# Output projection by head pairs in seven block products, probabilities divided before rounding, values two heads later

## The chip, the core and the metric

The kernel runs on one core of a Trainium2 chip. Its engines work side by side, each through its own list of instructions: TensorE (PE) multiplies matrices, VectorE (DVE), ScalarE (ACT) and GpSimd (POOL) work element by element, SyncE (SP) issues the DMA transfers. They wait for each other by semaphores. SBUF is the memory on the chip, PSUM the eight banks into which TensorE writes. The metric is the time of one execution on the device, in microseconds.

## The reference, cut to what matters

A layer of latent attention and a gated feed-forward block (FFN) on an input of 8 x 512 x 512, in fp32, with random weights. Each of the 8 batches is independent:

```
x = x + attention(layernorm(x))
x = x + ffn(layernorm(x))
# attention, 16 heads, D_QK = 128 + 64, D_V = 128
q  = rmsnorm(h @ wq_a.T, q_norm_w) @ wq_b.T                # rope on the last 64 of each head
kv = h @ wkv_a.T;  kv_c = rmsnorm(kv[..., :128]);  k_pe = rope(kv[..., 128:])
k_nope, v = split(kv_c @ wkv_b.T)
attn = softmax(q @ k.T / sqrt(192))
out  = (attn @ v) @ wo.T                                    # 2048 -> 512
# ffn, 512 -> 1536 -> 512, weights rounded to fp8
down(silu(gate(x)) * up(x))
```

## The kernel before

Every operand is held as two f16 halves, a high one (rounded) and a low one (the rest), and a product is three matmuls: high by high, high by low, low by high (`mul3`, L287 to 293). The kernel never forms keys or values of a head: the key half of `wkv_b` is multiplied into the query weights (`WAB`, "absorbed"), the value half into `wo` (`WVO`, 16 matrices of 128 x 512), so all heads share one latent key and value of 128 columns, and what the softmax weights is the latent row ("context").

A batch has 4 tiles of 128 rows and 16 heads. In head i (`head_step`) TensorE computes the scores of head i (20 matmuls of 512 columns into four PSUM banks), the values of head i - 1 (12), the absorbed queries of head i + 2 (9) and the projection of head i - 1 (12, `project_out`). VectorE takes the four row maxima of the scores (L1427, `maxima`), copies the context of head i - 1 out of PSUM and splits it (L1441, L1222), adds the four projected tiles into the residual `XR` times the reciprocal of the row's sum (L1449), and makes the low half of a query (L1222). ScalarE computes each tile's exponential twice, in fp32 with its sum (L1077) and in f16 (L1079), and GpSimd subtracts the one from the other (L1716). SyncE turns the f16 halves with transposing DMAs, and the values of a head wait for them. The order on every engine is written out in the code; a loop runs over pairs of heads in the middle. Between the attentions lies the FFN, with the next batch's queries and keys prepared beside it. Statistics and the norm of the next batch's rows are spread over the middle heads (`next_norm`). The latent products of the next batch (`latent`) stand between the last heads.

The change and the prediction touch: `scores`, `values`, `project_out`, `attention`, `end_of_attention` on TensorE; `probs`, `attention` on ScalarE; `context`, `add_out`, `head_step`, `attention`, `last_of_attention` on VectorE; `head`, `next_norm`, `attention` on GpSimd; `batch` on SyncE.

## Time and profile before

| | |
|---|---|
| time, median of 3 runs | 2231.03 us (2230.93 to 2232.12) |
| the profiled execution's span, first to last instruction | 2228.8 us, 2.2 us below the median |
| TensorE busy | 2205.4 us, 99%, 10977 matmuls |
| VectorE busy | 1557.8 us, 70% |
| ScalarE busy | 1066.6 us, 48% |
| GpSimd busy | 1001.5 us, 45% |
| share of TensorE in the chain that ended last | 93% |
| granted TensorE clock, mean | 0.999 of full speed |

Matmuls overlap: each is recorded with 379 ns for 512 columns, but one follows the other sooner, and what counts is the distance between two starts. In the timeline a row is: start, duration, engine, line, operation, output and inputs, shapes, and, in brackets, how long the engine had been idle before and what released it. `x4` joins four instructions of the same kind that follow without a gap; the duration is then that of the run.

### The profile page before, as it was taken

Reading aid. Unit: us, or ns where it says so; the run is one execution under the profiler, and the core shown is the slowest. Engines: PE = TensorE matmul, PEld = TensorE weight load, DVE = VectorE, ACT = ScalarE, POOL = GpSimd, SP = SyncE. Lnnn points to the kernel's source line nnn. Section 1 sums busy time; section 2 is a strip of 40 time slices with the busy share of each in tenths; the row PEclk is TensorE's granted clock in tenths of the full one; section 3 lists DMA queues with packets and bytes.
Section 4 is the critical chain, followed back from the end, with each engine's and each line's share of the span. In section 5 each row is a group of like instructions: output and inputs, shape, how many; then the busy total and the mean of one; then the engine's idle time right before and its main releaser. Section 6 shows DMA issues by size and latency. Waiting matters only on the chain.

```text
span 2228.8 us, 34908 instructions
## 1 busy us (share of the span) xinstructions
PE 2205.4 (99%) x10977; PEld 1026.8 (46%) x10977; DVE 1557.8 (70%) x3227; ACT 1066.6 (48%) x2345; POOL 1001.5 (45%) x688
## 2 busy tenths in 40 slices
PE   7999999999999999999999999999999999999999
PEld 5444544445444454444544445444454445444454
DVE  7888887776477764777648775587755877467773
ACT  6667564554255542555325553355443554345532
POOL 4657465453355524454244642536334363343322
PEclk9999999999999999999999999999999999999999
DMA  7868336562175631756216561365614564145530
GB/s 248 188 124 150 88 71 142 106 124 51 23 151 105 122 53 34 145 105 127 44 43 146 106 121 29 73 123 106 118 25 104 106 115 95 24 104 109 106 65 19
DMA packets 703800, 219.42 MB, mean 98 GB/s; under 512 B 685520, under 2 KB 685776, under 8 KB 702672
## 3 DMA queue, kind: packets, MB, share of 16 engines
q1 hardware_dynamic: 703696, 218.09, 47.7%
q8 instruction: 59, 0.97, 0.2%
q14 instruction: 45, 0.37, 0.0%
HBM read 40.78 MB, written 8.39 MB: 22 GB/s over the span
## 4 chain that ended last, share of the span: by engine, by line
PE 93%; DVE 3%; ACT 1%; DMA 1%; POOL 1%; issue 1%; SPq 0%; DVEq 0%; POOLq 0%
PE bank L853 13%; PE bank L291 11%; PE bank L293 11%; PE bank L292 11%; PE scores L863 7%; PE scores L663 5%; PE scores L293 5%; PE scores L291 5%; PE scores L292 5%; PE bank L674 4%; PE bank L675 4%; PE bank L676 4%; PE scores L660 3%; PE bank L840 1%; PE bank L689 1%; PE scores L557 1%
## 5 line engine op out<-in xcount | busy, mean ns | idle before, releaser
L1716 POOL TENSOR_TENSOR arena<-arena 128x1024 f16<-128x1024 f32 x256 | 545.7, 2132 | 620.3 <-ACT arena L1079 620.3
L1077 ACT ACTIVATE arena<-scores,shift 128x512 f32<-128x512 f32 x512 | 357.5, 698 | 535.0 <-DVE shift L1429 494.8
L1449 DVE SCALAR_TENSOR_TENSOR arena<-bank,rden,arena 128x512 f32<-128x512 f32 x508 | 347.9, 743 | 137.0 <-PE bank L293 137.0
L1427 DVE TENSOR_REDUCE mx<-scores 128x1 f32<-128x512 f32 x512 | 352.5, 689 | 20.5 <-PE scores L293 16.7
L1079 ACT ACTIVATE arena<-scores,shift 128x512 f16<-128x512 f32 x512 | 358.6, 700 | 0.0
L853 PE MATMUL bank<-arena,WFF 128*128 128x512 f16 x1392 | 313.5, 379 | 0.8 <-DVE arena L1601 0.6
L1774 POOL TENSOR_TENSOR arena<-arena 128x512 f16<-128x512 f32 x96 | 114.4, 1191 | 255.6 <-ACT arena L1152 255.6
L853 PEld LDWEIGHTS bank<-arena,WFF 128*128 128x128 f16 x1392 | 135.9, 98 | 164.1 <-DVE arena L1601 2.3
L291 PE MATMUL bank<-WVO,arena 128*128 (+1 forms) x512 | 194.2, 379 | 2.4 <-DVE arena L1222 1.2
L1222 DVE SCALAR_TENSOR_TENSOR arena<-bank,arena 128x512 f16<-128x512 f32 (+1 forms) x263 | 176.2, 670 | 29.1 <-ACT arena L1070 24.4
L663 PE MATMUL scores<-arena 128*128 128x512 f16 x512 | 195.4, 382 | 0.0
L292 PE MATMUL bank<-WVO,arena 128*128 (+1 forms) x512 | 194.1, 379 | 0.0
L291 PE MATMUL scores<-arena 128*128 128x512 f16 x512 | 194.0, 379 | 0.0
L292 PE MATMUL scores<-arena 128*128 128x512 f16 x512 | 194.0, 379 | 0.0
L293 PE MATMUL scores<-arena 128*128 128x512 f16 x512 | 194.0, 379 | 0.0
L293 PE MATMUL bank<-WVO,arena 128*128 (+1 forms) x512 | 194.0, 379 | 0.0
L674 PE MATMUL bank<-arena 128*128 128x512 f16 x476 | 180.4, 379 | 1.9 <-DMA arena<-arena 1.7
L676 PE MATMUL bank<-arena 128*128 128x512 f16 x476 | 180.4, 379 | 0.0
L675 PE MATMUL bank<-arena 128*128 128x512 f16 x476 | 180.4, 379 | 0.0
L1441 DVE TENSOR_SCALAR arena<-bank 128x512 f16<-128x512 f32 (+1 forms) x135 | 89.0, 660 | 130.1 <-PE bank L676 125.7
L863 PE MATMUL scores<-WFF,arena 128*128 128x512 f16 x752 | 177.6, 379 | 0.0
L1601 DVE SCALAR_TENSOR_TENSOR arena<-arena,bank 128x512 f32<-128x512 f32 x96 | 65.9, 687 | 158.5 <-ACT arena L1146 158.4
(159 smaller groups left out, 3480.5 us busy)
## 6 DMA issues: line engine op xcount, KB each, us to landing
arena<-arena SPq DMA_TRANSPOSE x712, 3.2
arena<-w_ffn SPq DMA_DIRECT2D x24, 384.0 KB, 3.5
arena<-x SPq DMA_DIRECT2D x8, 1024.0 KB, 5.6
out<-arena SPq DMA_DIRECT2D x32, 256.0 KB, 2.0
arena<-x SPq DMA_DIRECT2D x14, 512.0 KB, 4.4
WVO<-w_o SPq DMA_DIRECT2D x4, 1024.0 KB, 8.2
arena<-w_nope SPq DMA_DIRECT2D x4, 768.0 KB, 9.1
arena<-down_scale SPq DMA_DIRECT2D x8, 256.0 KB, 3.3
```

What stands on the lines that cost most here:

```text
L291: pe.matmul(dst, lhsT=ls(0), rhs=rs(0), start=first, stop=False)
L292: pe.matmul(dst, lhsT=ls(0), rhs=rs(1), start=False, stop=False)
L293: return pe.matmul(dst, lhsT=ls(1), rhs=rs(0), start=False, stop=last)
L663: pe.matmul(dst, lhsT=Q1[:, par, tile(t)], rhs=KA[:, :], start=False, stop=False)
L674: pe.matmul(dst[:, :], lhsT=KV[:, 0, j, :], rhs=PT[:, par, 0, :, j, :], start=(j == 0), stop=False)
L853: m = pe.matmul(dst[:, :], lhsT=w[:, c, k, :], rhs=XT[:, p, k, :], start=(k == 0 and p == 0), stop=(k == NK - 1 and p == 1))
L863: m = pe.matmul(SC[:, t, :], lhsT=FU[:, c % 4, p, tile(t)], rhs=WD[:, c, :], start=(c == 0 and p == 0), stop=(c == NF - 1 and p == 1))
L1077: act.activation(P32[:, t, :], SC[:, t, :], ACT.Exp, scale=EXP_SCALE, bias=shift[:, t:t + 1], accum_out=esum[:, par, t:t + 1]).then_inc(s[ ...
L1079: act.activation(PH[:, par, t, :], SC[:, t, :], ACT.Exp, scale=EXP_SCALE, bias=shift[:, t:t + 1]).then_inc(s["ph"], 1)
L1427: dve.tensor_reduce(mx[:, t:t + 1], SC[:, t, :], AX_X, ALU.max).then_inc(s["mxr"], 1)
L1449: dve.scalar_tensor_tensor(out=XR[:, t, :], in0=banks[t][:, :], scalar=by[:, t:t + 1], in1=XR[:, t, :], op0=ALU.mult, op1=ALU.add).then_in ...
L1716: pool.tensor_tensor(PL[:, par, two, :], P32[:, two, :], PH[:, par, two, :], ALU.subtract).then_inc(s["pl"], 1)
```

## The change

From batch 2 on (`B_PLAIN = 2`), heads 0 to 13 form seven pairs. For a pair the contexts of the even head (E) and the odd one (O) stand side by side against their two weight matrices stacked; rows are cut in two (tiles 0, 1 and tiles 2, 3), the output columns in two. That is a product of 2 x 2 blocks by 2 x 2 blocks, and it is computed by seven block products and sums of blocks (Winograd's form of Strassen's method) instead of eight. A block product (`duo_product`) is two tiles by three matmuls of 256 columns. Heads 14 and 15 keep the old projection.

- The sums of weight blocks (T1 to T4) are computed once, on GpSimd in batch 1 (`block_sums`), split into halves, and written to DRAM with the plain blocks (`w_duo`); from then on each pair's seven blocks are read from there, four early and three late (`early_blocks`, `late_blocks`), into the space of the old matrices.
- The sums of context blocks (S1 to S4) are made on GpSimd in the odd heads (`context_sums`).
- Since contexts of two heads are added, the probabilities must be divided by their sums first. ScalarE now computes four exponentials (fp32), VectorE the reciprocals, and ScalarE then scales them: three tiles are copied twice (f16 and fp32, in place), the fourth is multiplied on GpSimd (`nm3`) and copied once (`probs_divided`, `head_divided`).
- The context leaves PSUM in fp32 (`context_rows`), ScalarE makes its f16 half (`context_hi`), VectorE the low half (`context_lo`).
- VectorE adds eight blocks of 128 x 512 elements a pair into `XR` (`add_block`).
- Values of head i - 2, not i - 1, are computed in head i, and scores wait for the fp32 exponentials (`ex`) alone.
- From batch 1 on the norm of the next batch's rows is done on VectorE (`next_rows`) and rounded on ScalarE (`next_rows_hi`), where GpSimd did both.
- TensorE's and ScalarE's loops over pairs are written out.

```diff
+B_PLAIN = 2
+N_DUO = NH // 2 - 1
+HB = H // 2
+N_BLK = 7
+W_B11, W_B21, W_T1, W_T2, W_T3, W_T4, W_B22 = range(N_BLK)
+N_EARLY = 4
+X_E1, X_O1, X_O2, X_S3, X_S1, X_S2, X_S4 = range(N_BLK)
+EARLY = [(X_E1, W_B11, 0, True), (X_O1, W_B21, 2, True), (X_S1, W_T1, 1, True), (X_S2, W_T2, 0, False)]
+LATE = [(X_S3, W_T3, 0, False), (X_S4, W_B22, 1, False), (X_O2, W_T4, 2, True)]
+ADDS = [(0, 0, 0), (2, 0, 0), (1, 1, 1), (0, 0, 1), (0, 1, 0), (0, 1, 1), (1, 0, 1), (2, 1, 0)]
...
+            def duo_head(b, i):
+
+                if i < NH - 2:
+                    sp.wait_ge(s["sp"], NT * (b * NH + i) + NT)
+                    rope_rows(i + 2, i % 2)
+                if i >= 2:
+                    sp.wait_ge(s["ctp"], b * N_CT + i - 1)
+                    sp.sem_inc(s["turn"])
+                for half in range(2):
+                    prob_rows_hi(b * NH + i, i % 2, half)
+                    prob_rows_lo(b * NH + i, i % 2, half)
...
+                    if b >= B_PLAIN and 0 < pair * 2 + par < NH - 1:
+                        pe.wait_ge(s["ex"], g * NT + (t - NT + 1))
...
+            def duo_product(j, x, w, k, start):
+
+                for t in range(2):
+                    dst = DBANK[k][:, t * HB:(t + 1) * HB]
+                    for m, (p, q) in enumerate(((0, 0), (0, 1), (1, 0))):
+                        r = pe.matmul(dst, lhsT=XP[j % 2][:, p, x, tile(t)], rhs=WB[:, q, w, :],
+                                      start=(start and t == 0 and m == 0), stop=(m == 2), skip_group_check=True)
+                return r
+
+            def duo_early(b, j, parts=(0, 1)):
+
+                n, base = (b - B_PLAIN) * N_DUO + j + 1, order_of_duo(b, j)
+                for k, (x, w, bk, start) in enumerate(EARLY):
+                    if (k > 0) not in parts:
+                        continue
+                    if k == 0:
+                        pe.wait_ge(s["w_early"], 16 * n)
+                        pe.wait_ge(s["ctl"], b * N_CT + 2 * j + 2)
+                        pe.wait_ge(s["outr"], base)
+                    if x == X_S1:
+                        pe.wait_ge(s["x_lo"], n)
+                    if x == X_O1:
+                        pe.wait_ge(s["cth"], b * N_CT + min(2 * j + 3, 2 * N_DUO))
+                    if x == X_S2:
+                        pe.wait_ge(s["outr"], base + 1)
+                    duo_product(j, x, w, bk, start).then_inc(s["outp"], 1)
+
+            def duo_late(b, j):
+
+                n, base = (b - B_PLAIN) * N_DUO + j + 1, order_of_duo(b, j)
+                pe.wait_ge(s["w_late"], 16 * n)
+                pe.wait_ge(s["outr"], base + 4)
+                for k, (x, w, bk, start) in enumerate(LATE):
+                    if x == X_O2:
+                        pe.wait_ge(s["cth"], b * N_CT + min(2 * j + 4, 2 * N_DUO))
+                    duo_product(j, x, w, bk, start).then_inc(s["outp"], 2 if x == X_S3 else 1)
+
+            def duo_step(b, i):
+
+                scores(b, i // 2, i % 2)
+                if i >= 2:
+                    values(b, i // 2 - 1, i % 2)
+                if i >= 4 and i % 2 == 0:
+                    duo_early(b, (i - 4) // 2, (0,))
+                absorb(i + 2, b * NH + i + 2)
+                if i >= 4 and i % 2 == 0:
+                    duo_early(b, (i - 4) // 2, (1,))
+                elif i >= 5:
+                    duo_late(b, (i - 5) // 2)
...
+            def probs_divided(b, i):
+
+                g, par, n = b * NH + i, i % 2, (b - B_PLAIN) * (2 * N_DUO) + i
+                for t in range(NT):
+                    act.wait_ge(s["shift"], NT * g + t + 1)
+                    if i > 0 and t % 2 == 0:
+                        act.wait_ge(s["pl"], 2 * g - 1 + t // 2)
+                    act.activation(P32[:, t, :], SC[:, t, :], ACT.Exp, scale=EXP_SCALE, bias=shift[:, t:t + 1],
+                                   accum_out=esum[:, par, t:t + 1]).then_inc(s["ex"], 1)
+                for t in range(NT):
+                    if t % 2 == 0:
+                        act.wait_ge(s["rdn"], 2 * n + 1 + t // 2)
+                        if i >= 2:
+                            act.wait_ge(p_t[par][t // 2], halves_landed(b, i))
+                    act.wait_ge(s["ex"], NT * g + t + 1)
+                    if t == NT - 1:
+                        act.wait_ge(s["nm3"], n + 1)
+                        act.activation(PH[:, par, t, :], P32[:, t, :], ACT.Copy).then_inc(s["ph"], 1)
+                    else:
+                        act.activation(PH[:, par, t, :], P32[:, t, :], ACT.Copy,
+                                       scale=rden_duo[:, par, t:t + 1]).then_inc(s["ph"], 1)
+                        act.activation(P32[:, t, :], P32[:, t, :], ACT.Copy,
+                                       scale=rden_duo[:, par, t:t + 1]).then_inc(s["nm"], 1)
+                    if t == 1 and i >= 2:
+                        context_hi(b, i - 2)
...
+            def context_rows(b, i):
+
+                n, j, par = b * N_CT + i, i // 2, i % 2
+                dve.wait_ge(s["ctp"], n + 1)
+                k = (b - B_PLAIN) * N_DUO + j
+                if par == 0 and k > 0:
+                    dve.wait_ge(s["x_sum"], 5 * k)
+                if par and k > 0:
+                    dve.wait_ge(s["x_lo"], k)
+                x = X32[:, X_O1:X_O2 + 1] if par else XE
+                dve.tensor_scalar(x, BC[:, :].rearrange("p (m n) -> p m n", m=2), 1.0 / NS, None,
+                                  ALU.mult).then_inc(s["cth"], 1)
+
+            def context_lo(b, i):
+
+                j, par = i // 2, i % 2
+                dve.wait_ge(s["x_hi"], (b - B_PLAIN) * 2 * N_DUO + i + 1)
+                if par:
+                    x = slice(X_O1, X_O2 + 1)
+                    dve.tensor_tensor(XP[j % 2][:, 1, x], X32[:, x], XP[j % 2][:, 0, x], ALU.subtract).then_inc(s["ctl"], 1)
+                else:
+                    dve.tensor_tensor(XP[j % 2][:, 1, X_E1], XE[:, 0], XP[j % 2][:, 0, X_E1],
+                                      ALU.subtract).then_inc(s["ctl"], 1)
...
+                bk, i, n = ADDS[k]
+                to = XR[:, 2 * i:2 * i + 2, n * HB:(n + 1) * HB]
+                dve.scalar_tensor_tensor(out=to, in0=DBANK[bk][:, :].rearrange("p (t n) -> p t n", t=2),
+                                         scalar=1.0 / (KS * VS), in1=to, op0=ALU.mult, op1=ALU.add).then_inc(s["outr"], 1)
...
+            def duo_adds(b, j, ks):
+                for k in ks:
+                    add_block(b, j, k)
+
+            def duo_step(b, i, part=None):
+
+                g = b * NH + i
+                maxima(g)
+                reciprocals(b, i)
+                if i >= 2:
+                    context_rows(b, i - 2)
+                if i >= 4 and i % 2 == 0:
+                    duo_adds(b, (i - 4) // 2, (0,))
+                if i >= 2:
+                    context_lo(b, i - 2)
+                if part in (0, 1, 2):
+                    next_norm(b, part)
+                if i >= 4 and i % 2 == 0:
+                    duo_adds(b, (i - 4) // 2, (1, 2, 3))
+                elif i >= 5:
+                    duo_adds(b, (i - 5) // 2, (4, 5, 6, 7))
+                qa_lo(g + 2, i % 2)
+                if part in (2, 3):
+                    next_norm(b, part + 1)
...
+            def head_divided(b, i):
+
+                g, par, n = b * NH + i, i % 2, (b - B_PLAIN) * (2 * N_DUO) + i
+                pool.wait_ge(s["ex"], NT * g + NT)
+                pool.wait_ge(s["rdn"], 2 * n + 2)
+                t = NT - 1
+                pool.tensor_tensor(P32[:, t, :], P32[:, t, :], rden_duo[:, par, t:t + 1].broadcast_to((P, S)),
+                                   ALU.mult).then_inc(s["nm3"], 1)
+                if i >= 3 and i % 2:
+                    context_sums(b, (i - 3) // 2)
+                for half in range(2):
+                    two = slice(2 * half, 2 * half + 2)
+                    pool.wait_ge(s["nm"], 3 * n + 2 + half)
+                    if half:
+                        pool.wait_ge(s["nm3"], n + 1)
+                    pool.wait_ge(s["ph"], NT * g + 2 * half + 2)
+                    pool.tensor_tensor(PL[:, par, two, :], P32[:, two, :], PH[:, par, two, :],
+                                       ALU.subtract).then_inc(s["pl"], 1)
+                    if i == 0:
+                        rotate(b, N_ROT_FFN + 1 + half)
+                if i >= 3 and i % 2:
+                    context_sums_rest(b, (i - 3) // 2)
...
+                x = [X32[:, m] for m in range(N_BLK)]
+                step(x[X_S1], XE[:, 1], x[X_O2], ALU.add, 0)
+                step(x[X_S3], XE[:, 0], XE[:, 1], ALU.subtract, 0)
+                step(x[X_S2], x[X_S1], XE[:, 0], ALU.subtract, 1)
+                step(x[X_S4], x[X_O1], x[X_S2], ALU.subtract, 3)
```

How the lists of instructions change, at three places. Names: `sp` scores done, `ex` exponential done, `ctp` values done, `outp` projected block done, `outr` block added, `qah` query's high half done, `x_hi` context's f16 half done, `x_lo` context sums split, `rdn` reciprocals done.

VectorE in a middle head before, after its four maxima (`bank` is PSUM, `arena` SBUF):

```order
L1434 TENSOR_SCALAR dsum<-esum 128x4 [waits ex]
L1436 RECIPROCAL rden<-dsum 128x4 [waits den]
L1441 TENSOR_SCALAR arena<-bank 128x512 [waits ctp]
L1222 SCALAR_TENSOR_TENSOR arena<-bank,arena 128x512 [waits cth]
L1449 SCALAR_TENSOR_TENSOR arena<-bank,rden,arena 128x512 [waits outp,rden]
L1449 SCALAR_TENSOR_TENSOR arena<-bank,rden,arena 128x512 [waits outp] x3
L1222 SCALAR_TENSOR_TENSOR arena<-bank,arena 128x512 [waits qah]
```

And now, in an even head:

```order
L1737 TENSOR_SCALAR dsum_duo<-esum 128x2 [waits ex]
L1739 RECIPROCAL rden_duo<-dsum_duo 128x2 [waits dsn]
L1737 TENSOR_SCALAR dsum_duo<-esum 128x2 [waits ex]
L1739 RECIPROCAL rden_duo<-dsum_duo 128x2 [waits dsn]
L1751 TENSOR_SCALAR arena<-bank 128x512 [waits x_sum,ctp]
L1777 SCALAR_TENSOR_TENSOR arena<-bank,arena 128x2x256 [waits outr,outp]
L1762 TENSOR_TENSOR WVO<-arena,WVO 128x256 [waits x_hi]
L1777 SCALAR_TENSOR_TENSOR arena<-bank,arena 128x2x256 [waits outr,outp]
L1777 SCALAR_TENSOR_TENSOR arena<-bank,arena 128x2x256 [waits outp] x2
L1487 SCALAR_TENSOR_TENSOR arena<-bank,arena 128x512 [waits qah]
```

Reciprocals of the same head, which wait for its last exponentials, now stand ahead of the context; the context's low half reads SBUF only and waits for ScalarE (`x_hi`); adds are split by it.

ScalarE in a head before, each tile's two exponentials (`REGISTER_ALU` only sets up a wait):

```order
L1077 ACTIVATE arena,esum<-scores,shift 128x512 [waits pl]
L1079 ACTIVATE arena<-scores,shift 128x512
L1074 REGISTER_ALU
L1077 ACTIVATE arena,esum<-scores,shift 128x512 [waits shift]
L1079 ACTIVATE arena<-scores,shift 128x512
L1074 REGISTER_ALU
L1077 ACTIVATE arena,esum<-scores,shift 128x512 [waits pl,shift]
L1079 ACTIVATE arena<-scores,shift 128x512
L1074 REGISTER_ALU
L1077 ACTIVATE arena,esum<-scores,shift 128x512 [waits shift]
L1079 ACTIVATE arena<-scores,shift 128x512
```

And now, after four exponentials of an even head:

```order
L1294 ACTIVATE arena<-arena,rden_duo 128x512 [waits ex,p_t00]
L1296 ACTIVATE arena<-arena,rden_duo 128x512
L1294 ACTIVATE arena<-arena,rden_duo 128x512 [waits ex]
L1296 ACTIVATE arena<-arena,rden_duo 128x512
L1322 REGISTER_ALU
L1324 REGISTER_ALU [waits cth]
L1325 ACTIVATE WVO<-arena 128x256 [waits outp]
L1286 REGISTER_ALU
L1294 ACTIVATE arena<-arena,rden_duo 128x512 [waits ex,p_t01,rdn]
L1296 ACTIVATE arena<-arena,rden_duo 128x512
L1291 REGISTER_ALU [waits ex]
L1292 ACTIVATE arena<-arena 128x512 [waits nm3]
```

The second exponential from PSUM has become a run of seven copies within SBUF behind all four exponentials, with the copy of the context of head i - 2 in the middle.

TensorE at the end of a batch before, from the projection of head 14 to that of head 15 (L689 the values of head 15):

```order
L291 MATMUL bank<-WVO,arena 128x512 [waits outr]
L292 MATMUL bank<-WVO,arena 128x512
L293 MATMUL bank<-WVO,arena 128x512
L689 MATMUL bank<-arena 128x256 [waits ctl,p_t10]
L689 MATMUL bank<-arena 128x256 x11
L689 MATMUL bank<-arena 128x256 [waits outr,p_t11]
L689 MATMUL bank<-arena 128x256 x11
L291 MATMUL bank<-WVO,arena 128x512 [waits ctl,cth]
```

And now, between the projection of head 14 and the values of head 15:

```order
L874 MATMUL bank<-WVO 128x256 [waits outr,ctl,w_early]
L874 MATMUL bank<-WVO 128x256 x5
L874 MATMUL bank<-WVO 128x256 [waits cth]
L874 MATMUL bank<-WVO 128x256 x5
L874 MATMUL bank<-WVO 128x256 [waits x_lo]
L874 MATMUL bank<-WVO 128x256 x5
L874 MATMUL bank<-WVO 128x256 [waits outr]
L874 MATMUL bank<-WVO 128x256 x5
L874 MATMUL bank<-WVO 128x256 [waits outr,w_late]
L874 MATMUL bank<-WVO 128x256 x11
L874 MATMUL bank<-WVO 128x256 [waits cth]
L874 MATMUL bank<-WVO 128x256 x5
```

The last pair's seven products stand there, and the first of them waits for the adds of head 14 (`outr`), the fifth for its own pair's first four adds.

## Rows read from the trace of the kernel before

**Rows 1.** the page: busy time and share of the engines

```profile
PE 2205.4 (99%) x10977; PEld 1026.8 (46%) x10977; DVE 1557.8 (70%) x3227; ACT 1066.6 (48%) x2345; POOL 1001.5 (45%) x688
```

**Rows 2.** timeline, TensorE (start us, us): first score matmuls of two middle heads

```profile
1291.18 0.61 PE L660 MATMUL scores<-arena 64*128 64x512 f16 x4
1302.40 0.61 PE L660 MATMUL scores<-arena 64*128 64x512 f16 x4
```

**Rows 3.** timeline, TensorE: the same of heads 0 and 1, batch 3

```profile
886.62 0.60 PE L660 MATMUL scores<-arena 64*128 64x512 f16 x4
896.55 0.60 PE L660 MATMUL scores<-arena 64*128 64x512 f16 x4
```

**Rows 4.** timeline, TensorE: 12 projection matmuls, 24 matmuls of 256 columns, and the next

```profile
1062.26 0.38 PE L291 MATMUL bank<-WVO,arena 128*128 128x512 f16 x1
...
1064.85 2.78 PE L689 MATMUL bank<-arena 128*128 128x256 f16 x24
1067.47 0.38 PE L291 MATMUL bank<-WVO,arena 128*128 128x512 f16 x1
```

**Rows 5.** timeline, VectorE, a middle head after its last maximum

```profile
1307.40 0.16 DVE L1434 TENSOR_SCALAR dsum<-esum 128x4 f32<-128x4 f32 x1
1307.60 0.18 DVE L1436 RECIPROCAL rden<-dsum 128x4 f32<-128x4 f32 x1
1309.20 0.69 DVE L1441 TENSOR_SCALAR arena<-bank 128x512 f16<-128x512 f32 x1 [1.42 <-PE bank L676]
1309.92 0.69 DVE L1222 SCALAR_TENSOR_TENSOR arena<-bank,arena 128x512 f16<-128x512 f32 x1
1311.87 2.73 DVE L1449 SCALAR_TENSOR_TENSOR arena<-bank,rden,arena 128x512 f32<-128x512 f32 x4 [1.25 <-PE bank L293]
```

**Rows 6.** timeline, VectorE when it is behind: first maximum, fourth shift, head 1

```profile
898.85 0.68 DVE L1427 TENSOR_REDUCE mx<-scores 128x1 f32<-128x512 f32 x1
...
901.92 0.15 DVE L1429 TENSOR_SCALAR shift<-mx 128x1 f32<-128x1 f32 x1
```

**Rows 7.** timeline, ScalarE: exponentials and a query copy, middle head

```profile
1293.79 0.69 ACT L1077 ACTIVATE arena<-scores,shift 128x512 f32<-128x512 f32 x1 [4.50 <-DVE shift L1429]
1294.47 0.68 ACT L1079 ACTIVATE arena<-scores,shift 128x512 f16<-128x512 f32 x1
...
1299.92 0.60 ACT L1070 ACTIVATE arena<-bank 128x512 f16<-128x512 f32 x1 [1.03 <-PE bank L293]
```

**Rows 8.** timeline, ScalarE: copies out of SBUF, with a scale pointer (rs_s) and without

```profile
904.78 1.19 ACT L1037 ACTIVATE arena<-arena 128x512 f16<-128x512 f32 x2
1356.98 0.71 ACT L1032 ACTIVATE arena<-arena 128x256 f16<-128x256 f32 x2
1368.12 1.10 ACT L1027 ACTIVATE arena<-arena,rs_s 128x384 f16<-128x384 f32 x2
1373.37 1.26 ACT L1019 ACTIVATE arena<-arena,rs_s 128x128 f16<-128x128 f32 x4
```

**Rows 9.** timeline, VectorE: side work beside the heads

```profile
909.28 1.28 DVE L1380 TENSOR_TENSOR arena<-arena 128x512 f16<-128x512 f32 x2
...
935.50 1.25 DVE L1320 BATCH_NORM_STATS2 bn<-arena 128x6 f32<-128x512 f32 x2
...
1347.48 1.92 DVE L1301 TENSOR_SCALAR arena<-arena,mv,rs_y 128x512 f32<-128x512 f32 x4
```

**Rows 10.** source line L1380, VectorE, both inputs in SBUF: duration ns min/median/max

```profile
L1380 DVE TENSOR_TENSOR arena<-arena x64: 679/682/1693, 40.1 to 1994.5; 128x512 f16<-128x512 f32 x64
```

**Rows 11.** timeline: one such subtraction that met a GpSimd instruction

```profile
1168.54 0.84 POOL L1688 TENSOR_TENSOR arena<-arena 128x256 f32<-128x256 f32 x1
1168.87 1.06 DVE L1380 TENSOR_TENSOR arena<-arena 128x512 f16<-128x512 f32 x1
```

**Rows 12.** groups by line, GpSimd (xcount | busy us, mean ns | idle before)

```profile
L1716 POOL TENSOR_TENSOR arena<-arena 128x1024 f16<-128x1024 f32 x256 | 545.7, 2132 | 620.3 <-ACT arena L1079 620.3
L1743 POOL TENSOR_TENSOR arena<-arena 128x512 f16<-128x512 f32 x24 | 27.7, 1156 | 2.1
```

413 lines of the change are left out of this document (346 added, 67 removed).

## The prediction

> **What bounds the kernel now.** I read the page's table of engines first. TensorE is busy 99% of the span, VectorE 70%, ScalarE 48%, GpSimd 45% [rows 1]: one queue of matmuls sets the time, and the others may be late only as long as TensorE still has something to do. So the questions are what a matmul costs and how far the other engines are from making it wait. The timeline of TensorE gives the first: the score matmuls of two middle heads are 11.22 us apart [rows 2], 12 projection matmuls take 2.59 us (0.216 each), 24 matmuls of 256 columns 2.62 us (0.109 each) [rows 4]. Half the columns cost half the time; narrow products are not penalised. The second comes from VectorE's timeline in a middle head: it waits twice for TensorE, 1.42 and 1.25 us [rows 5], so it has 2.7 us to spare in 11.22. At a batch's start it is already tight: the first maximum of head 1 starts at 898.85, 2.3 us after that head's first score matmul [rows 3, 6], where the first tile of scores needs about 1.5.
>
> **What the change takes off TensorE.** A pair of heads now costs 7 products of 6 matmuls of 256 columns, 42 x 0.109 = 4.59 us, where two projections cost 24 x 0.216 = 5.18. That is 0.59 us a pair, for 7 pairs in 6 batches 24.8 us, 4.1 us a batch. All other matmuls stay.
>
> **What it lays on the chain of the other engines.** In head i VectorE makes four maxima and shifts, ScalarE four exponentials; then ScalarE scales and copies, and VectorE may not start the maxima of head i+1 before it has done what stands in its queue, which waits for ScalarE. I call the distance from first maximum to first maximum a link, and work out its length if TensorE never holds it up:
> - Maxima and shifts 3.22 us (898.85 to 901.92 + 0.15) [rows 6].
> - Shift to exponential 0.12, and the last exponential with its sum 0.68 until the next instruction [rows 7].
> - Seven copies of 128x512 follow, in place of the four second exponentials, which ran in between. Two plain copies of 512 columns take 1.19 us, two of 256 0.71, so two of 384 would take 0.95; with a scale pointer they take 1.10 [rows 8], 0.07 more each. A plain copy follows another by 0.54 (1.19 less the last one's own 0.65), one with a pointer by 0.61: 6 x 0.61 + 0.54 = 4.20.
> - The query copy 0.60 [rows 7] and VectorE's subtraction behind it 0.65.
>
> That is 9.5 us, with the context copy (0.3 or 0.55, even and odd heads) 9.8 and 10.0. From head 4 on another way through the same queues is longer: after four copies (2.44) and the context copy (0.41 or 0.63) VectorE subtracts (0.43 or 0.71), adds 3 or 4 blocks at 0.66 (four took 2.73) [rows 5] and does the query's subtraction (0.60): 9.9 in an even head, 11.0 in an odd one. TensorE's work is 11.25 and 10.6 (11.22 less 2.59, plus 4 or 3 products of 0.65). Sum of a pair: chain 20.9, TensorE 21.85. It would hold, with 0.9 us to spare in two heads instead of 5.3.
>
> **Two things take that away.** First, values come two heads later, so TensorE's heads 1, 2 and 3 have nothing to project: 9.93 less 3.89 for the two rotations gives 6.04 for head 1, 8.63 for heads 2 and 3, against links of 9.5, 9.8 and 10.0, with 0.9 more in heads 2 and 3 for a rotation's subtraction (0.60 alone [rows 9], 0.3 for a port). Second, the context subtraction has both inputs in SBUF and stands beside GpSimd, which is now busy 17 of 22 us: a multiplication of 512 columns (about 1.2), two subtractions of 1024 (2.13 each) in each head, and in odd ones four sums of 256 (0.68 each by the line through 1156 ns at 512 and 2132 at 1024 columns [rows 12]), a copy and another 2.13. The trace has this meeting: L1380 takes 682 ns in the median and 1693 at most [rows 10]; one that began at 1168.87 under a GpSimd instruction that ran until 1169.38 ended at 1169.93, 0.55 behind it [rows 11]. It stood still until the other was done. In an even head the context subtraction becomes ready some 0.3 us after GpSimd began a 2.13 us subtraction (both follow the fourth copy), so it waits about 1.6; in an odd head it meets one of the 0.7 us sums and waits about 0.4. Links with blocks become 11.5 and 11.4, the pair 22.9, a little over TensorE's 21.85. Bounds of that wait: 0 and 2.13 in a head.
>
> A page of the Trainium skill speaks against this change here: "SBUF — State Buffer", section "Who interferes with whom", says that a VectorE instruction with two SBUF inputs contends with a GpSimd instruction that reads SBUF, and that whoever issues first has the port for its whole instruction. By that rule, the trace agrees ([rows 11]). Its "VectorE in 2-port mode" clause would hold up the row normalisations too, which this change moves to VectorE; no row shows one beside GpSimd.
>
> On the copies, "ScalarE: Activation LUTs", section "What ACT_TABLE_LOAD costs", gives 93 ns for each pointer operand, where the rows give 70; by the page the link would be 0.14 us longer.
>
> **The lateness, added up.** TensorE must wait when the second product of an even head finds the context of head i-2 not copied out: it comes 9.28 us into the head, the copy ends 3.22 + 0.95 + 0.30 + 0.79 = 5.26 us after the first maximum. So a lateness up to 4.0 us costs nothing, and all that is beyond it, at its highest, is lost once. Lateness = sum of links less TensorE's work:
> - Head 1: 2.5. Head 2: + 9.5 - 6.04 = 5.9. Head 3: + 10.7 - 8.63 = 7.9. Head 4: + 10.9 - 8.63 = 10.2.
> - Heads 5 to 8 also carry the next batch's statistics (1.2 for a pair of tiles [rows 9], 0.2 for each of nine small steps, 0.4 for merging): 10.2 + 12.7 - 11.25 = 11.7; + 12.6 - 10.6 = 13.7; + 13.1 - 11.25 = 15.5; + 13.0 - 10.6 = 17.9.
> - Heads 8 to 11 come behind a row normalisation (0.46 alone, four took 1.92 [rows 9], and 0.5 for the port, chosen between 0 and 2.13): 19.1, 20.9, 22.1; head 12: 22.9.
>
> So 18.9 us of waits. At the end of a batch three new ones: pair 6 stands directly behind head 14's projection, waits for its last add (0.12 + 0.74 + 0.10, 0.9 us), its second half waits for its own fourth add (0.9 again), and head 15's third tile waits for a context that VectorE takes up behind two more adds (0.6): 2.4. A batch with a successor: 18.9 + 2.4 - 4.1 = +17.2, five of them +86. The last batch has no next normalisation; its pairs gain 1.05 each: 10.2 at head 4, 14.4 at head 12, so 10.4 + 2.4 - 4.1, and 1.8 because two residual adds and statistics now come behind the last context instead of before it: +10.5. Batch 1: GpSimd's ten sums (7 to 8 us) push its next subtraction back by 1.5, and the transposes behind it had some 2 to spare; 0 to 2, I take 1. Weight blocks (0.9 MB a pair) are asked for over ten us before use: nothing. Sum: +97.5 us; the profiled span becomes 2228.8 + 97.5 = 2326.3, the median, 2.2 us above the span today, 2328.5.
>
> **The rivals.**
> A. *The chain as above, but the port costs little.* For it: 682 ns is the median in [rows 10]; against it: GpSimd was idle most of the time there. Then the pair of links is 20.9, lateness peaks at 12.7 (9.6 at head 4, 11.0 at 6, 12.7 at 8), the waits are 8.7: 8.7 + 2.4 - 4.1 = +7.0 five times, +5.5 in the last batch, +1: 2272.5.
> B. *Faster.* One mechanism: the copies are shorter than I have them. The lateness of heads 1 to 4 shrinks by 0.07 us for each 0.01 us off a copy and head; from a spacing of 0.35 us down it stays below 4 at head 4, and the pairs gain. Then TensorE keeps 24.8 less the 14 us at the batches' ends, about 2220; all waits gone, 2206. Against it: the plain copies of [rows 8] follow each other by 0.54, and nothing there is shorter.
> C. *No change:* rival A with copies at about 0.40, where 4.1 us gained and the waits cancel. It needs a coincidence.
> D. *Dearer:* copies at 0.66, or port waits near 2 us also for rotations and normalisations: 4 to 6 us more a batch, 2355 to 2365.
>
> **How the numbers follow.** Forecast 0.60, A 0.22, B 0.08, C 0.03, D 0.07. The range 2258 to 2355 goes from A with plain copies (2 us less a batch) to the foot of D and leaves out B, C and half of D, about 0.15. What this kernel's measurement can tell from no change is 0.2%, 4.5 us: faster 0.08, same 0.03, slower 0.89.
>
> **What would show it.** TensorE busy about 1.1% less in us, and its share from 99% to 94 or 95%. In each batch from 2 on, waits of TensorE for VectorE's context rows in even heads: none before head 2, the largest (3 to 4 us) in head 4, then 1 to 3 in heads 6 to 10; three below 1 us at the end. Head starts in batch 3 further apart than 11 us from 4 to 11, at 10.9 on average in 12 and 13. The context subtraction with a mean well over its 0.68 and 0.42, near 2 us in even heads. Batch 1 unchanged within 2 us. I am wrong if TensorE's waits sit elsewhere (for a transpose or a weight block), if the context subtraction keeps its short time (rival A), or if heads 2 to 4 start 8.6 us apart (rival B).

## The result, and the profile after

The changed kernel takes 2357.8 us (median of 4 runs, 2357.35 to 2358.5) against 2231.3 us before: ratio 1.0567, 95% interval 1.0555 to 1.058. It is 126.5 us slower; the forecast was 97.5 us slower, and the time lies 2.8 us above its range. The profiled execution has a span of 2355.5 us.

The page's engines and chain, to be held against [rows 1]:

```profile
PE 2229.0 (95%) x11733; PEld 1109.1 (47%) x11733; DVE 1687.2 (72%) x3419; ACT 1295.5 (55%) x2712; POOL 1357.3 (58%) x1053
...
PE 56%; DVE 20%; ACT 10%; issue 8%; POOL 3%; DMA 2%; SPq 1%; ACTq 0%; DVEq 0%; POOLq 0%
```

TensorE's share fell from 99% to 95%, and the chain that ended last, 93% TensorE before, is 56%. The two waits that are largest (engine, line, waited for: us in total, times, longest):

```profile
PE bank L874 <- DVE arena L1751: 56.3, 24, 5.4
...
PE scores L763 <- ACT arena L1282: 14.4, 35, 0.8
```

L874 is a block product, L1751 VectorE's copy of an even head's context out of PSUM (`context_rows`), whose bank that product writes next. L1282 is an exponential: at the start of heads 2 to 4 TensorE waits until it has read the bank that the scores go into. Where the time goes by batch, from the distances of their first score matmuls (batch 3 from 911.21 to 1205.88; L660 before, L763 now):

| | before | after | difference | forecast |
|---|---|---|---|---|
| batch 1 | 271.20 | 273.92 | +2.7 | +1 |
| batches 2 to 6, each | 271.0 to 271.4 | 292.6, 294.7, 294.3, 294.2, 294.1 | +22.8 on average | +17.2 |
| batch 7 to the end | 257.6 | 267.1 | +9.5 | +10.5 |

So the middle batches hold the whole miss: 5 x 5.6 = 28 us. One of them, TensorE's timeline in head 4 of batch 3 and its wait in head 8:

```profile
911.21 0.60 PE L763 MATMUL scores<-arena 64*128 64x512 f16 x4
...
957.62 0.38 PE L335 MATMUL bank<-arena,WAB 128*128 128x512 f16 x1
962.26 4.02 PE L874 MATMUL bank<-WVO 128*128 128x256 f16 x18 [4.25 <-DVE arena L1751]
966.21 1.04 PE L763 MATMUL scores<-arena 64*128 64x512 f16 x4
...
1016.29 0.61 PE L874 MATMUL bank<-WVO 128*128 128x256 f16 x2 [5.42 <-DVE arena L1751]
```

Between the two, 54 us in which VectorE falls behind again. A bracket is idle time; from start to start the wait is 962.26 - 957.62 - 0.22 = 4.42, 0.17 more. The 18 matmuls (three block products) behind it take 4.02 us, where 24 took 2.62 before [rows 4]. The granted clock tells why (window: us, TensorE busy, clock, DMA share, GB/s):

```profile
961.00:968.00 7.00, 5.74 (x24) 0.52 0.54 105
1016.00:1019.00 3.00, 2.71 (x13) 0.50 0.47 46
```

The clock, 2.4 GHz otherwise, stood at 1.2 GHz behind each of the two long waits, and came back while TensorE worked; over the kernel it was low for 66 us. The forecast had not thought of that.

VectorE and GpSimd in head 4, from its first maximum:

```profile
956.09 0.68 DVE L1699 TENSOR_REDUCE mx<-scores 128x1 f32<-128x512 f32 x1
...
960.15 1.24 DVE L1737 TENSOR_SCALAR dsum_duo<-esum 128x2 f32<-128x2 f32 x1 [0.57 <-ACT arena L1282]
961.43 0.17 DVE L1739 RECIPROCAL rden_duo<-dsum_duo 128x2 f32<-128x2 f32 x1
961.51 0.69 DVE L1751 TENSOR_SCALAR arena<-bank 128x512 f32<-128x512 f32 x1
...
962.90 2.23 DVE L1762 TENSOR_TENSOR WVO<-arena,WVO 128x256 f16<-128x256 f32 x1
```

```profile
959.21 2.16 POOL L2234 TENSOR_TENSOR WVO<-WVO 128x1024 f16<-128x1024 f32 x1
961.67 1.04 POOL L2183 TENSOR_TENSOR arena<-arena,rden_duo 128x512 f32<-128x512 f32 x1 [0.31 <-DVE rden_duo L1739]
962.72 4.40 POOL L2193 TENSOR_TENSOR arena<-arena 128x1024 f16<-128x1024 f32 x2
```

The context subtraction (L1762) stands still beside GpSimd, as forecast. But so does a multiplication of two numbers per partition: L1737 begins at 960.15 and ends at 961.39, with GpSimd's L2234 (961.37), and the copy that TensorE waits for comes behind it. In head 7:

```profile
1005.93 1.87 DVE L1529 TENSOR_TENSOR rs_t<-rs_y 128x4 f32<-128x4 f32 x1
1007.84 0.94 DVE L1539 SCALAR_TENSOR_TENSOR rs_t<-rs_t,rs_v 128x4 f32<-128x4 f32 x1
1008.82 0.16 DVE L1542 SCALAR_TENSOR_TENSOR rs_x<-rs_t,rs_y 128x4 f32<-128x4 f32 x1
1009.09 2.17 DVE L1601 TENSOR_SCALAR arena<-arena,mv,rs_x 128x512 f32<-128x512 f32 x1
1011.18 0.68 DVE L1699 TENSOR_REDUCE mx<-scores 128x1 f32<-128x512 f32 x1
```

```profile
1003.57 4.22 POOL L2193 TENSOR_TENSOR arena<-arena 128x1024 f16<-128x1024 f32 x2
1007.72 1.05 POOL L2232 CAST WVO<-WVO 128x1024 f16<-128x1024 f32 x1
1008.85 2.13 POOL L2234 TENSOR_TENSOR WVO<-WVO 128x1024 f16<-128x1024 f32 x1
```

Three steps (L1529, L1539, L1601) that take 0.16, 0.16 and 0.53 alone took 4.98 us: 4.1 us of standing still in one link. The first ends with GpSimd's L2193 (1007.80 and 1007.79), the second with its L2232 (1008.78 and 1008.77). By source line (duration ns min/median/max):

```profile
L1737 DVE TENSOR_SCALAR dsum_duo<-esum x168: 147/169/1929, 623.6 to 2236.1; 128x2 f32<-128x2 f32 x168
L1762 DVE TENSOR_TENSOR WVO<-arena,WVO x42: 414/2229/2236, 647.5 to 2249.0; 128x256 f16<-128x256 f32 x42
L1601 DVE TENSOR_SCALAR arena<-arena,mv,rs_x x24: 529/1008/2171, 434.9 to 1930.1; 128x512 f32<-128x512 f32 x24
L1701 DVE TENSOR_SCALAR shift<-mx x512: 153/154/156, 58.9 to 2255.7; 128x1 f32<-128x1 f32 x171
L1739 DVE RECIPROCAL rden_duo<-dsum_duo x168: 165/166/168, 623.8 to 2236.4; 128x2 f32<-128x2 f32 x168
L1777 DVE SCALAR_TENSOR_TENSOR arena<-bank,arena x336: 672/680/693, 669.5 to 2275.1; 128x512 f32<-128x512 f32 x168
```

What matters is which maxima lie far above the minima. Held were instructions with both inputs in SBUF (L1762), and multiplications with one input there and more than one column (L1737, L1601). Never held were those of one column (L1701), the reciprocal (L1739), and an instruction with an input from PSUM (L1777). The Trainium skill, "SBUF — State Buffer", section "Who interferes with whom", says that a VectorE instruction with one source in SBUF contends with GpSimd too when it runs in a 2-port mode. By its "VectorE: DVE Perf Modes", section "Mode 2×_2P — use both read ports for one tensor", that mode wants the outermost dimension longer than one to be even, or odd and the same in source and destination; a single column has no such dimension. The trace agrees: two columns were held for up to 1929 ns (L1737), one column never took more than 156 ns (L1701). The forecast cited the first of these pages and still priced only the subtraction and, at 0.5 us, the normalisation.

### The profile page after: what moved, and what is told of

Read it like the earlier page. It is cut to its first block, busy times and chain, and to the rows that moved or that the text cites. A ratio compares the mean times of both kernels' runs of the same rounds, so it can differ in the third digit from the quotient of the medians.

```text
span 2355.5 us, 37234 instructions
## 1 busy us (share of the span) xinstructions
PE 2229.0 (95%) x11733; PEld 1109.1 (47%) x11733; DVE 1687.2 (72%) x3419; ACT 1295.5 (55%) x2712; POOL 1357.3 (58%) x1053
## 4 chain that ended last, share of the span: by engine, by line
PE 56%; DVE 20%; ACT 10%; issue 8%; POOL 3%; DMA 2%; SPq 1%; ACTq 0%; DVEq 0%; POOLq 0%
PE bank L1044 12%; PE scores L1054 7%; DVE mx L1699 5%; PE bank L333 4%; PE bank L335 4%; PE bank L334 4%; PE bank L874 4%; DVE arena L1777 4%; ACT arena L1296 3%; ACT arena L1294 2%; PE scores L333 2%; PE scores L335 2%; PE scores L334 2%; PE bank L784 2%; PE scores L766 2%
## 5 line engine op out<-in xcount | busy, mean ns | idle before, releaser
L2193 POOL TENSOR_TENSOR arena<-arena 128x1024 f16<-128x1024 f32 x168 | 366.9, 2203 | 42.7 <-ACT arena L1296 42.6
L1699 DVE TENSOR_REDUCE mx<-scores 128x1 f32<-128x512 f32 x512 | 349.2, 682 | 6.8 <-PE scores L335 6.3
L1282 ACT ACTIVATE arena<-scores,shift 128x512 f32<-128x512 f32 x336 | 230.7, 687 | 223.4 <-DVE shift L1701 184.5
L874 PE MATMUL bank<-WVO 128*128 128x256 f16 x1764 | 229.2, 285 | 73.8 <-DVE arena L1751 56.3
L874 PEld LDWEIGHTS bank<-WVO 128*128 128x128 f16 x1764 | 176.8, 102 | 134.8 <-DVE arena L1751 68.5
L2110 POOL TENSOR_TENSOR arena<-arena 128x1024 f16<-128x1024 f32 x88 | 188.9, 2154 | 85.3 <-ACT arena L1272 85.3
L1777 DVE SCALAR_TENSOR_TENSOR arena<-bank,arena 128x512 f32<-128x512 f32 x336 | 212.6, 680 | 13.1 <-PE bank L874 12.0
L2183 POOL TENSOR_TENSOR arena<-arena,rden_duo 128x512 f32<-128x512 f32 x84 | 87.3, 1039 | 224.4 <-DVE rden_duo L1739 224.4
L766 PE MATMUL scores<-arena 128*128 128x512 f16 x512 | 198.3, 387 | 0.0
L333 PE MATMUL scores<-arena 128*128 128x512 f16 x512 | 197.0, 385 | 0.0
L334 PE MATMUL scores<-arena 128*128 128x512 f16 x512 | 196.1, 383 | 0.0
L335 PE MATMUL scores<-arena 128*128 128x512 f16 x512 | 195.8, 382 | 0.0
L1294 ACT ACTIVATE arena<-arena,rden_duo 128x512 f16<-128x512 f32 x252 | 178.8, 709 | 8.2 <-DVE rden_duo L1739 7.9
L1296 ACT ACTIVATE arena<-arena,rden_duo 128x512 f32<-128x512 f32 x252 | 178.7, 709 | 0.0
```

Source lines behind the costliest of these rows:

```text
L333: pe.matmul(dst, lhsT=ls(0), rhs=rs(0), start=first, stop=False)
L334: pe.matmul(dst, lhsT=ls(0), rhs=rs(1), start=False, stop=False)
L335: return pe.matmul(dst, lhsT=ls(1), rhs=rs(0), start=False, stop=last)
L766: pe.matmul(dst, lhsT=Q1[:, par, tile(t)], rhs=KA[:, :], start=False, stop=False)
L874: r = pe.matmul(dst, lhsT=XP[j % 2][:, p, x, tile(t)], rhs=WB[:, q, w, :], start=(start and t == 0 and m == 0), stop=(m == 2), skip_group_ ...
L1282: act.activation(P32[:, t, :], SC[:, t, :], ACT.Exp, scale=EXP_SCALE, bias=shift[:, t:t + 1], accum_out=esum[:, par, t:t + 1]).then_inc(s[ ...
```

## The experiments

There are two theories of the missing 29 us. Port: VectorE's queue sets the time, and its steps stand still beside GpSimd for longer than I had it. Clock: the stretches at 1.2 GHz cost it. All ratios are to the kernel before, with their 95% interval; the changed kernel is 1.0567.

**TensorE's waits filled.**

```diff
+                if i in (4, 8):
+                    for _ in range(18 if i == 4 else 22):
+                        pe.matmul(BT[:, :], lhsT=WG[:, 0, 0, :], rhs=WD[:, 0, :], start=True, stop=True)
                 if i >= 4 and i % 2 == 0:
                     duo_early(b, (i - 4) // 2, (1,))
```

> The changed kernel with idle TensorE time filled: in heads 4 and 8 of every batch from 2 on, 18 and 22 matmuls of 512 columns (0.216 us each, 3.9 and 4.8 us) stand right before the product that waits 4.3 and 5.4 us for VectorE's context rows; their result is overwritten. Two theories of the 29 us that the forecast lacks. Port: VectorE's queue sets the time up to head 12, because GpSimd holds up its steps for longer than I took; what TensorE does in those waits, and at which clock it runs behind them, costs nothing. Then 2355 to 2362, no gain. Clock: the granted clock is 0.5 in 66 us of the changed kernel, always behind such a wait, which is 33 us of matmuls; with the waits filled most of that comes back: 2325 to 2338. In both the stretches at 0.5 behind heads 4 and 8 should go from the trace.

Measured 2362.65 us, ratio 1.0585 (1.0567 to 1.0602), 0.65 above the range of the port theory. The mean granted clock:

```profile
core 0: 2359.9 us, clock 0.996
```

It was 0.986. The stretches behind the waits of heads 4 and 8 are gone (20.6 us at 1.2 GHz are left, at head 4's start and behind a wait in head 10), yet batches 3 to 6 start 294.1 to 294.2 us apart, as they did (294.1 to 294.7): head 10 of batch 3 now waits 2.3 us instead of 1.6, and VectorE's links from head 7 on are the same. The 5 us more are the last batch, where head 8 has no wait to fill. The clock theory falls for the middle batches: there the slow stretches lie beside a chain that is late anyway.

**The same ahead of head 4.**

```diff
+                if i in (2, 3):
+                    for _ in range(24):
+                        pe.matmul(BT[:, :], lhsT=WG[:, 0, 0, :], rhs=WD[:, 0, :], start=True, stop=True)
                 absorb(i + 2, b * NH + i + 2)
```

> The changed kernel with 24 matmuls of 512 columns (5.2 us) more in each of heads 2 and 3 of every batch from 2 on, as much as the four projections before had that heads 1 to 3 no longer have; their result is overwritten. 62 us of TensorE's work in all. If the lateness up to head 4 is all VectorE's and ScalarE's, these fill the waits that heads 2 to 4 have now (2.5 and 4.3 us a batch) and the stretch at half clock behind them (3.4 us): 2355 to 2368. If TensorE's work counts there: 2420.

Measured 2376.9 us, ratio 1.065 (1.0633 to 1.0668), 9 us above the range for filled waits and 43 below full price: of 62 us of work 19 show, 2.2 on average in each of batches 2 to 6 and 9.4 in the last. TensorE's wait at head 4 is gone, and head 8's is still 5.4 us: most of the work went where TensorE would have waited. But in head 3 it overran. Link 3 (first maximum of head 3 to that of head 4) is 13.4 us, TensorE's length now, instead of 11.3, and those 2 us stay. In the last batch VectorE, once late, stayed late: its even links are 12.7 us there, 11.0 in the changed kernel. The rows of head 10 show why, the changed kernel's first, then this run's:

```profile
2184.38 0.42 DVE L1762 TENSOR_TENSOR WVO<-arena,WVO 128x256 f16<-128x256 f32 x1
2184.40 4.48 POOL L2193 TENSOR_TENSOR arena<-arena 128x1024 f16<-128x1024 f32 x2
```

```profile
2200.33 2.15 DVE L1765 TENSOR_TENSOR WVO<-arena,WVO 128x256 f16<-128x256 f32 x1 [1.47 <-ACT WVO L1328]
2200.07 4.41 POOL L2196 TENSOR_TENSOR arena<-arena 128x1024 f16<-128x1024 f32 x2 [1.23 <-ACT arena L1299]
```

VectorE on time begins the context subtraction 0.02 us before GpSimd's and takes 0.41 or 0.42 us in heads 6 to 12; VectorE late begins it 0.26 us after and takes 2.15 in each even head up to 12, which is the 1.7 us by which those links are longer. So lateness brings the wait for GpSimd, and that wait keeps VectorE late.

**GpSimd's subtractions cut to an eighth.**

```diff
-                    pool.tensor_tensor(PL[:, par, two, :], P32[:, two, :], PH[:, par, two, :],
+                    pool.tensor_tensor(PL[:, par, two, 0:64], P32[:, two, 0:64], PH[:, par, two, 0:64],
```

> The changed kernel with GpSimd's two subtractions of 1024 columns in each divided head cut to 128 (64 of each tile); left out is the rest of the probabilities' low halves, in whose place the high halves are transposed, so all transfers and matmuls stay. GpSimd's multiplication of 512 columns and its sums of contexts stay. Port: of the 23.8 us by which VectorE's instructions in batch 3 exceed their own shortest forms some 15 to 20 go, TensorE's waits sink to about 9 to 11 us a batch: 2270 to 2300. Clock: the waits shrink only by what the forecast had for the context subtractions alone (some 7 us a batch), and the stretches at the lower clock stay: 2310 to 2325.

The edit also lets SyncE transpose the high halves in the place of the low ones, which are left out. Measured 2300.2 us, ratio 1.0302 (1.0285 to 1.0319), 0.2 above what the port theory gave and 10 below the other's range. The two-number multiplication is never held now:

```profile
L1737 DVE TENSOR_SCALAR dsum_duo<-esum x168: 158/164/171, 622.5 to 2179.2; 128x2 f32<-128x2 f32 x168
```

So GpSimd's subtractions cost 57.6 us, 10.7 in a middle batch. GpSimd is not idle in this run: it is busy half the time in heads 4 to 11 (70% in the changed kernel), and it still holds VectorE, 1.65 us for L1529 in head 7 and 2.09 for the sums of head 14 (`sums_of_head`, L1706, 128x4, 0.16 alone). What stays, 12.1 a batch, is in two waits of 2.8 us in heads 4 and 8 with their slow stretches, and in the batch's end.

**One column instead of two.**

```diff
-                    dve.tensor_scalar(dsum_duo[:, par, two], esum[:, par, two], 1.0 / NS, None, ALU.mult).then_inc(s["dsn"], 1)
...
+                    for t in (2 * half, 2 * half + 1):
+                        dve.tensor_scalar(dsum_duo[:, par, t:t + 1], esum[:, par, t:t + 1], 1.0 / NS, None,
+                                          ALU.mult).then_inc(s["dsn"], 1)
```

> The changed kernel with the multiplication of two sums at once (128x2, mean 338 ns, at most 1.93 us) done as two multiplications of one column (128x1); nothing left out. The shifts have that form and take 0.15 us each time, whatever GpSimd does. Port, by form: 4.7 us of VectorE's 23.8 us of delay in batch 3 go, at most 2 x 0.08 us a head come in: 2 to 3.5 us a batch less, 2341 to 2348. If a VectorE instruction of one column is held up as well: 2358 to 2364. Clock: no change, 2355 to 2360.

Measured 2351.6 us, ratio 1.0533 (1.0515 to 1.0551). 336 instructions, none of them held:

```profile
L1738 DVE TENSOR_SCALAR dsum_duo<-esum x336: 142/144/156, 621.1 to 2229.9; 128x1 f32<-128x1 f32 x168
```

That is the clearest proof of the form, since nothing else changed. The gain is 6 us, not 10 to 17. The 4 to 5 us a batch for which this multiplication stood still are gone, but link 4 stays at 12.69 (12.68): the context subtraction waits for ScalarE's copy and then for GpSimd's subtraction that begins just ahead of it, and so ends 9.05 us after the first maximum, as before (9.04). What is gained is the copy ahead of it, for which TensorE waits.

**Row normalisations on GpSimd again.**

```diff
-                        if 7 <= i < 7 + NT and not last:
-                            next_rows(b, i - 7)
...
+                        if 8 <= i < 8 + NT and not last:
+                            rows_normalised(b, i - 8)
                         head_divided(b, i)
...
+                pool.tensor_scalar(XN[:, t, :], XN[:, t, :], mv[:, t, 0:1], rs_x[:, t:t + 1], ALU.subtract,
+                                   ALU.mult).then_inc(s["x32"], 1)
```

> The changed kernel with the normalisation of the next batch's rows back on GpSimd in batches from 2 on (one head later, heads 8 to 11, ahead of that head's multiplication, where GpSimd idles 2.6 us); nothing left out. Port: VectorE loses four steps that took 5.3 us a batch with their delays (0.53 each alone), in heads 7 to 10, all of them ahead of TensorE's last wait for it in head 12: 3 to 5 us a batch less, 2332 to 2343, if GpSimd's new 1.1 us instructions don't hold up others for as much. Clock: no more than 1 us a batch: 2350 to 2358.

Measured 2343.4 us, ratio 1.0491 (1.0473 to 1.0508), at the upper end of the port theory's range: 14 us less. Head 8's wait is 3.3 us instead of 5.4.

**GpSimd's subtractions in halves.**

```diff
-                    pool.tensor_tensor(PL[:, par, two, :], P32[:, two, :], PH[:, par, two, :],
-                                       ALU.subtract).then_inc(s["pl"], 1)
+                    for u in (2 * half, 2 * half + 1):
+                        r = pool.tensor_tensor(PL[:, par, u, :], P32[:, u, :], PH[:, par, u, :], ALU.subtract)
+                    r.then_inc(s["pl"], 1)
```

> The changed kernel with GpSimd's subtractions of 1024 columns (2.13 us alone) cut into two of 512 (1.16 us) in the divided heads; nothing left out, GpSimd has 0.4 us more to do in a head. If a VectorE step is held until the GpSimd instruction that it met has ended, it now waits for at most 1.2 us there instead of 2.1: a third to a half of the delays that meet these subtractions goes, 3 to 6 us a batch: 2325 to 2342. If it is held until GpSimd's whole run of instructions is over, or GpSimd's own lateness counts: 2355 to 2362.

Measured 2354.5 us, ratio 1.0551 (1.0533 to 1.0569): only 3 us, hardly more than the intervals can tell. The first row is the context subtraction, the others head 7:

```profile
L1762 DVE TENSOR_TENSOR WVO<-arena,WVO x42: 415/1255/2159, 647.6 to 2246.4; 128x256 f16<-128x256 f32 x42
```

```profile
1004.58 1.04 DVE L1529 TENSOR_TENSOR rs_t<-rs_y 128x4 f32<-128x4 f32 x1
1005.65 1.08 DVE L1539 SCALAR_TENSOR_TENSOR rs_t<-rs_t,rs_v 128x4 f32<-128x4 f32 x1
1006.76 0.94 DVE L1542 SCALAR_TENSOR_TENSOR rs_x<-rs_t,rs_y 128x4 f32<-128x4 f32 x1
1007.81 2.36 DVE L1601 TENSOR_SCALAR arena<-arena,mv,rs_x 128x512 f32<-128x512 f32 x1
```

One step alone waits half as long (1255 ns in the median, 2229 before). But in a run of small steps every one now meets the next piece, where before the first two took nearly the whole wait. A hold ends with the GpSimd instruction, as expected; that it then comes again for the next step was not.

**The last three edits together.**

> The changed kernel with sums of one column, row normalisations back on GpSimd and its subtractions in pieces of 512 columns, together; nothing left out. The first two gave 6 and 14 us; with 3 to 6 us a batch for the pieces: 2310 to 2325. If the three take away the same delays: 2335 to 2345.

Measured 2322.6 us, ratio 1.0408 (1.039 to 1.0425): within its range and 35 us less than the changed kernel, more than the 24 of the three alone. That the last held step before a wait was another one in each of them would explain it, but no run shows that.

**The statistics one head later**, without and with the halved subtractions (against the edits together above).

```diff
-                start = 4 if first or b >= B_PLAIN else 3
+                start = 5 if b >= B_PLAIN else 4 if first else 3
...
-                        if 8 <= i < 8 + NT and not last:
-                            rows_normalised(b, i - 8)
+                        if 9 <= i < 9 + NT and not last:
+                            rows_normalised(b, i - 9)
```

> Sums of one column, row normalisations on GpSimd, and the next batch's statistics one head later (heads 5 to 8 instead of 4 to 7, the normalisations in heads 9 to 12), so that the last small steps stand in an even head, where GpSimd idles; its subtractions whole (1024 columns); nothing left out. The two first gave 6 and 14 us; the small steps lose up to 2.5 us of delay a batch: 2322 to 2332. If delays only move to other steps: 2338.

> The same with GpSimd's subtractions in pieces of 512 columns. Against the combination without the shift (2322.6): three of its small steps in head 7 met a piece each (3.0 us a batch together), which now stand where GpSimd idles: 2305 to 2314. If delays only move: 2320 to 2325.

Measured 2382.7 us (1.0671, 1.0654 to 1.0689) and 2370.1 us (1.0624, 1.0606 to 1.0642): both far off. Heads 13 and 14 of batch 4 take 27.8 us in the first, 21.9 in the three edits together. TensorE now waits for transposes that it did not wait for:

```profile
PE bank L784 <- DMA arena<-arena: 21.5, 14, 3.1
```

By the order of the lists the last rounded row comes in head 12, SyncE's transposes of these rows wait for it, and behind them stand those of head 13's probabilities. And the shift had left a part of the small steps in head 7. So these runs say nothing of the times for which VectorE is held.

**The small steps where GpSimd idles.**

```diff
-                if part in (2, 3):
-                    next_norm(b, part + 1)
+                if part == 2:
+                    next_norm(b, 3)
+                    next_norm(b, 4)
```

> The changed kernel with the last six of the next batch's small steps (128x4) done at the end of head 6 instead of head 7; nothing left out. In head 7 two of them took 1.87 and 0.94 us beside GpSimd, instead of 0.16 each; at the end of head 6 GpSimd idles from 992.9 to 999.4. If VectorE's delays by GpSimd up to the wait in head 8 are what the forecast lacks: 2.5 us a batch less, 2345 (2341 to 2350). If a delay taken away there comes back at the next step that GpSimd can hold: 2353 to 2358.

Measured 2346.35 us, ratio 1.051 (1.0492 to 1.0528), on the forecast. The two steps that took 1.87 and 0.94:

```profile
993.38 0.16 DVE L1529 TENSOR_TENSOR rs_t<-rs_y 128x4 f32<-128x4 f32 x1
993.58 0.16 DVE L1539 SCALAR_TENSOR_TENSOR rs_t<-rs_t,rs_v 128x4 f32<-128x4 f32 x1
...
1005.06 2.13 DVE L1601 TENSOR_SCALAR arena<-arena,mv,rs_x 128x512 f32<-128x512 f32 x1
```

Link 7 is 13.15 us instead of 16.33, head 8's wait 2.3 to 2.7 us instead of 5.4.

The same with the three edits that are together above:

> Sums of one column, row normalisations on GpSimd, its subtractions in pieces of 512 columns (2322.6 together), and the small steps at the end of head 6 as well; nothing left out. In that combination four of them in head 7 had 3.0 us of delay a batch: 2309 (2304 to 2315). If the delay only moves: 2320 to 2325.

Measured 2310.5 us, ratio 1.035 (1.0333 to 1.0368), again as expected, and the best version that leaves nothing out. It is still 79 us slower than the kernel before.

**Without ScalarE's float32 copies.**

```diff
-                        act.activation(P32[:, t, :], P32[:, t, :], ACT.Copy,
-                                       scale=rden_duo[:, par, t:t + 1]).then_inc(s["nm"], 1)
```

> The changed kernel without ScalarE's three scaled copies in float32 (left out: the low half of tiles 0 to 2 is taken from undivided exponentials). ScalarE's run behind the exponentials is 3 x 0.61 = 1.83 us shorter, GpSimd's subtractions start earlier. By the chain of waits: lateness grows by 1.2 to 1.8 us less in each of heads 1 to 4, so head 4 waits for at most 1 us, and afterwards a link is shorter than TensorE's head unless GpSimd holds it up: waits of 0 to 5 us a batch, 2215 to 2245. If the port alone were what costs (ScalarE's copies hidden behind it): above 2320.

Measured 2334.3 us, ratio 1.0461 (1.0444 to 1.0479): 23 us less, where I had 113 to 143. Lateness at head 4 did fall (5.4 us instead of 9.4), yet TensorE waits there for 4.3 us. ScalarE's wait is new:

```profile
951.24 0.69 ACT L1282 ACTIVATE arena<-scores,shift 128x512 f32<-128x512 f32 x1 [3.50 <-POOL arena L2190]
```

The exponentials overwrite what GpSimd's subtractions (L2190) of the head before still read. With ScalarE out of the way GpSimd's own work is the next chain.

**Both left out.**

> Both leaner engines at once: GpSimd's subtractions cut to 128 columns and ScalarE's three scaled float32 copies left out (left out: the low halves, in whose place the high halves are transposed). Without the copies alone the exponentials of head 4 waited 3.5 us for GpSimd's subtractions, without the subtractions alone the lateness at heads 4 and 8 was still 8.7 and 7.2 us. Together every link should be at most TensorE's head: no wait over 1 us, TensorE's saving is there (24.8 us) less the batches' ends (2.4 each) and batch 1 (2.7): 2215 to 2228. If something else of the change holds TensorE up: above 2245.

Measured 2242.0 us, ratio 1.0048 (1.0032 to 1.0065), between the two ranges given. The granted clock is 1.0, the largest wait in heads 1 to 13 is 1.1 us (head 8). Middle batches take 272.95 us, still 1.8 more than before: the 4.1 us that seven products save are outweighed by the batch's end, where TensorE waits 1.36, 1.08, 0.91 and 0.40 (and 0.16 more each), and by 1.6 us in heads 2 and 8. The 1.36 stands behind one more hold, the 2.09 us of `sums_of_head`, which takes 0.69 there in the changed kernel. So even with the chain gone up to head 13 the change is no gain.

**Six matmuls more in each pair.**

```diff
                     if x == X_S1:
+                        for _ in range(6):
+                            pe.matmul(BT[:, 0:HB], lhsT=WG[:, 0, 0, :], rhs=WD[:, 0, 0:HB], start=True, stop=True)
                         pe.wait_ge(s["x_lo"], n)
```

> The changed kernel with 6 more matmuls of 256 columns (0.65 us) in every pair of heads of the batches from 2 on, as many as the eighth product would take; their result is overwritten. If VectorE's queue sets the time up to head 12, only the two pairs behind it lose, 1.3 us in five batches, and in the last batch, where TensorE waits for nothing after head 4, six pairs or so: 2366 (2362 to 2370). If TensorE's saved matmuls shorten the kernel as they stand, 42 pairs x 0.65 = 27 us: 2385.

Measured 2379.0 us, ratio 1.0665 (1.0647 to 1.0683): 21 us, where I had 8 and the full price is 27. Up to head 13 the expectation holds in the middle batches: of 3.3 us of added matmuls 0.3 to 1.3 show, 0.7 on average. The rest, 2.1 us in each of them, comes in head 15: 0.65 is the last pair's matmuls, 1.5 a wait that the changed kernel does not have there (VectorE, GpSimd, TensorE in batch 3):

```profile
1103.36 2.09 DVE L1708 TENSOR_SCALAR dsum<-esum 128x4 f32<-128x4 f32 x1
1102.85 2.58 POOL L2112 TENSOR_TENSOR arena<-arena 128x1024 f16<-128x1024 f32 x1
1107.07 0.38 PE L333 MATMUL bank<-WVO,arena 128*128 128x512 f16 x1 [1.36 <-DVE arena L1719]
```

The four sums of head 14 (`sums_of_head`) meet GpSimd's subtraction at its start and take 2.09 us, 0.69 in the changed kernel, and the context copy for which TensorE waits (L1719) stands behind them. In the last batch 4.6 us show up to head 13, 1.8 in head 4 and then 0.66, the full price, in each even head: TensorE's own length sets the time there. So my expectation was right in that TensorE's work beside a late chain is nearly free, and wrong in that it left out what the shift of a fraction of a microsecond does to the next hold.

## Why the forecast was right in kind and 29 us short

The mechanism was right: TensorE waits in even heads from head 4 on for VectorE's copy of the context, because the start of a batch has nothing to project and the links of the other engines' chain are longer than TensorE's heads. Link by link in batch 3 (first maximum to first maximum, L1699):

| head | 1 | 2 | 3 | 4 | 5 | 6 | 7 | 8 | 9 | 10 | 11 |
|---|---|---|---|---|---|---|---|---|---|---|---|
| forecast | 9.5 | 10.7 | 10.9 | 12.7 | 12.6 | 13.1 | 13.0 | 12.45 | 12.4 | 12.45 | 11.4 |
| measured | 9.35 | 11.51 | 11.31 | 12.68 | 12.11 | 13.97 | 16.33 | 11.82 | 13.13 | 11.83 | 11.07 |

- *The links' plain parts* (maxima 3.22, copies 0.61 apart, query copy) were right: head 1 has nearly nothing else and is 0.15 us off. The copy without a scale pointer was mis-sized: it takes 616 ns where one with a pointer takes 709, 93 apart and not the 70 that I took from the rows, and the next instruction follows it by 0.52, not 0.54.
- *The context subtraction beside GpSimd*: forecast near 2 us in even heads, measured 1.86 on average, 2.23 in the median; in odd heads 1.03.
- **The step that failed** is the price of the other steps beside GpSimd: "0.2 for each of nine small steps" and "0.46 alone [...] and 0.5 for the port". In head 7 these three terms were 1.87, 0.94 and 2.17 us, and the link 3.3 us longer than forecast. The half sums were not priced at all: "a lateness up to 4.0 us costs nothing" took the copy to end 5.26 us after the first maximum, and it ends 6.11 us after (961.51 + 0.69 - 956.09), since L1737 is held for 1.1. Together with 0.8 and 0.4 in links 2 and 3 (rotations of 1.93 and 1.51 us, forecast 0.9) that makes TensorE 24.2 us late by head 13, not 18.9: 5.3 a batch. (The eleven links sum to 135.1 instead of 131.2, the later copy adds 0.85, and head 1 starts 0.3 later.) Of the kernel's time, the small steps moved took 11.5 us away, one column instead of two 6.2, the row normalisations on GpSimd 14.4.
- *The batch's end*: forecast 2.4 us of waits. Read: 1.08 and 0.91 as expected, 0.51 and 0.40 besides, and 0.16 for each: 3.5.

```profile
1106.78 2.78 PE L874 MATMUL bank<-WVO 128*128 128x256 f16 x24 [1.08 <-DVE arena L1728]
1110.47 2.12 PE L874 MATMUL bank<-WVO 128*128 128x256 f16 x18 [0.91 <-DVE arena L1777]
```

5.3 + 1.1 = 6.4, and batch 3 is 23.7 us longer, not 17.2. Over five batches (5.6 on average) that is the miss.

- *Where the waits sit*: forecast "the largest (3 to 4 us) in head 4, then 1 to 3 in heads 6 to 10"; there are 2.6 to 4.3 in head 4 and 5.4 in head 8, behind the long link 7. Waits that the forecast had nowhere: for exponentials at the start of heads 2 to 4 (0.2, 0.3 and 1.9 in batch 3), and about 1.1 in head 7.
- *The last batch* came to +9.5 (10.5 forecast) by luck. The forecast had 6.2 us lost by head 4 and 4.2 more by head 12, since the links with blocks were to be longer than TensorE's heads. Measured, TensorE is 9.9 us late when head 5 starts (heads 2 to 4 take 9.16, 10.10 and 19.16 where its work is 8.63, 8.63 and 11.25), about 1.5 of it by the clock of 1.2 GHz, and waits for nothing in heads 5 to 14: VectorE has caught up, its context subtraction takes 0.41 us in heads 6 to 12, and the forecast's 1.6 us of wait in each is not there.
- *Batch 1* +2.7 (0 to 2): TensorE waits for transposes, 0.5 and 0.6 us in heads 10 and 12 and 1.0 in head 15.
- *Rival A* (little cost of the port) is 28 us below even the kernel with GpSimd's subtractions cut to an eighth. *Rival B*'s 2206 to 2220 was not reached either: with the chain gone up to head 13 the kernel takes 2242. *Rival D* named the right mechanism, "port waits near 2 us also for rotations and normalisations", and its 2355 to 2365 holds the time; I gave it 0.07.
- *The clock* was missing among the rivals; the run with the waits filled shows that it would have added nothing in the middle batches.

Left open: how the 12.1 us that remain with GpSimd's subtractions cut divide between the plain links, the holds that are left and the slow stretches behind the waits, which no run separated; and why the three edits together gain more than their sum.

## What to carry to other kernels

When work moves to GpSimd, go through VectorE's list beside it and mark every instruction with two SBUF inputs, and every multiplication of more than one column with one, whatever its size: each can wait for the rest of a GpSimd instruction, and a run of small ones should stand where GpSimd idles. Whether a step is held hangs on which engine begins first, so a small shift elsewhere can bring a hold or take it away. A saving on the busiest engine is worth something only if the other engines' chain from step to step stays shorter than that engine's own; write that chain down link by link, starting where the busiest engine has least to do. Don't read a slower clock as a cost before the waits beside it have been filled once.

## What the hardware showed that I had not expected

- A VectorE multiplication of 128x2 took up to 1.93 us beside GpSimd, one of 128x4 2.09 us, one of 128x1 never more than 0.156 us in 336.
- The same context subtraction took 0.42 us when it began 0.02 us before GpSimd's instruction, and 2.15 us when it began 0.26 us after.
- Halving the GpSimd instructions halved one step's wait (2229 to 1255 ns) and left a run of three small steps as slow as before (3.06 us, 2.97 before).
- TensorE's clock stood at 1.2 GHz behind waits of 2.6 to 5.4 us, and in batches 4 to 6 also among four waits of 0.2 to 0.8 us at head 4's start, for 3 to 7 us each time, 66 us in all; with the long waits filled the kernel was no faster.
- A wait of TensorE cost 0.17 us more, from start to start, than the idle time shown (4.42 against 4.25).
